# A two-layer decoder with a hand-ordered instruction list: filler matmuls in the last part of TensorE's list, and new orders for four engines

## The chip, the cores and the metric

The kernel runs on one core of a Trainium2 chip. A core has four engines that compute, each with its own instruction queue worked off strictly in order: TensorE (PE, matmuls and transposes; PEld is its weight load), VectorE (DVE), ScalarE (ACT) and GpSimd (POOL). SyncE (SP) issues the DMAs. They synchronise by semaphores alone. The metric is the device time of one execution in microseconds, lower is better.

## The reference

Input are 32 sequences of 128 rows with 256 channels, and a context of the same shape. Six sublayers follow each other, each as x = layernorm(x + f(x)):

```python
x = _layernorm(x + _L0_attn_ref(x, ...))        # 16 heads, window of 7 keys, extra weights per window place
x = _layernorm(x + _L0_xattn_ref(x, ctx, ...))  # one-head attention on the context
x = _layernorm(x + _L0_ffn_ref(x, ...))         # 8 experts, each takes its 16 best rows, attends among them
x = _layernorm(x + _L1_attn_ref(x, ...))        # one-head attention, scores times a decay mask
x = _layernorm(x + _L1_xattn_ref(x, ctx, ...))  # row of context chosen by argmax, then 16-head attention
x = _layernorm(x + _L1_ffn_ref(x, ...))         # 256 -> 1024 -> conv of 3 -> silu -> 256, rounded to 8 bits / 3 values
```

All sequences are independent of each other until the end.

## The kernel before

The sequences are worked in 16 groups (`NG`) of two (`GB`), so a group is 256 rows. Every sublayer is a set of stations named by a letter: S setup (once), Q queries, keys and values and A the rest of the windowed attention; B cross attention; X and Y the two halves of the experts; C the decayed attention; D the choice of context rows and E the attention on them, T its output projection and norm; F the first part of the feed-forward, H its gating, second projection and norm. A station exists on each engine as a Python generator: at each `yield` it has issued one step, a few instructions with their semaphore waits and signals.

The order in which an engine issues steps is written out by hand as a string of letters in `ORDER`, one letter for a step. `walk` goes through it: a letter issues the next step of that station for its current group, and when a group's steps are used up, the station turns to the next group. So several groups are in flight at once, and what stands behind a waiting step in an engine's string waits with it.

I name a step by its letter, its group and its work. For TensorE these are, in the last part of its string:

- D15.kv, D15.xT, D15.q, D15.sc, D15.hotT, D15.v: projections, transposes and scores of the choice of group 15, in PSUM bank_c.
- E15.sc0, sc1 (scores of the two sequences, line 868), negT (transpose of the row maxima, line 876), lg0 and lg1 (logits, lines 889 and 893), val0 and val1 (values, in line 904's loop), tu0 and tu1 (turned back, line 909). E15.sc0 waits for `d_v_out` at 16. In groups 14 and 15, lg1 waits for all four exponentials of lg0, val1 for those of lg1.
- T15.aT and T15.wc (lines 922 and 930): transposes and output projection; behind them the norm of T15: sums on VectorE (line 1027), squares on ScalarE (line 1535), scale on GpSimd (lines 1841 to 1847), normalisation on ScalarE (line 1542).
- F15.rows (line 936), xqT (line 955), p0 to p3 (line 966), and for the last group t0 to t3 (line 975): scale rows, transposes of the rounded rows, four projections that share bank_f, and four transposes of the gated result. VectorE reads a projection out (ev, line 1424), convolves it (line 1433), gates it (line 1443) and takes maxima (line 1463).
- H14.topT, H14.rows, H14.out (lines 990, 994 and 1012): maximum and scale of group 14's hidden values, then 16 matmuls. VectorE makes the four parts that they read, n0 to n3 (line 1502). For group 15 there are H15.rows and four steps o0 to o3 of four matmuls (line 1005).

TensorE's string ends as follows, W aside: T14.wc, E15.sc0, H13.out, E15.sc1, F14.rows, F14.xqT, F14.p0, F14.p1, E15.negT, E15.lg0, F14.p2, E15.lg1, F14.p3, E15.val0, E15.val1, E15.tu0, E15.tu1, T15.aT, T15.wc, H14.topT, H14.rows, F15.rows, F15.xqT, F15.p0 to p3, F15.t0, F15.t1, H14.out, F15.t2, F15.t3, H15.rows, H15.o0 to o3.

The helpers `mm` (line 503), `project_rows` (line 513 its bias matmul), `to_channels` (534) and `turn_blocks` (539) issue most matmuls. `take` waits until a bank has been read out.

Of the kernel before, what the change touches and what calls it, by code (L numbers as in the profile page):

```python
# [67 lines left out]

ORDER = {
    "PE": (  # L70
        "QQQASSASASBQSQBAQAASDABABSBBQBQXBXASAXQXAXABXBABYBYQBYYYQYBAYAXQCXCABXBXAXBAXBQYCYQCYYYBYCAYCAXBXQDAXDXD"
# [1915 lines left out]
```

## Time and profile before

| | us |
|---|---|
| three runs | 1006.9, 1003.46, 1008.17 |
| median | 1006.9 |
| the profiled execution | 1006.9 |
| its span, first to last instruction | 1005.1 |
| TensorE busy in the span | 915.2 (91%) |
| VectorE busy | 855.5 (85%) |
| ScalarE busy | 738.8 (74%) |
| GpSimd busy | 218.2 (22%) |
| TensorE's mean granted clock | 0.964 |

All times are microseconds. "Clock" is the clock that the chip granted to TensorE, as a share of 2.4 GHz; it knows two levels, 1.00 and 0.50, and a value between them is a mean over a stretch. Ends of matmuls are modelled, so a matmul is shown a little longer than it holds the queue; the distance from one start to the next is the better measure. In a timeline, square brackets give the idle time of the engine before a group, and what ended it.

### The profile page before, as it was taken

Reading aid. Unit: us, or ns where it says so; the run is one execution under the profiler, and the core shown is the slowest. Engines: PE = TensorE matmul, PEld = TensorE weight load, DVE = VectorE, ACT = ScalarE, POOL = GpSimd, SP = SyncE. Lnnn points to the kernel's source line nnn. Section 1 sums busy time; section 2 is a strip of 40 time slices with the busy share of each in tenths; the row PEclk is TensorE's granted clock in tenths of the full one; section 3 lists DMA queues with packets and bytes.
Section 4 is the critical chain, followed back from the end, with each engine's and each line's share of the span. In section 5 each row is a group of like instructions: output and inputs, shape, how many; then the busy total and the mean of one; then the engine's idle time right before and its main releaser. Section 6 shows DMA issues by size and latency. Waiting matters only on the chain.

```text
span 1005.1 us, 20332 instructions
## 1 busy us (share of the span) xinstructions
PE 915.2 (91%) x7396; PEld 674.3 (67%) x7396; DVE 855.5 (85%) x2217; ACT 738.8 (74%) x1852; POOL 218.2 (22%) x469
## 2 busy tenths in 40 slices
PE   6888999999999999999999999999999999998654
PEld 4566676767777676767677676767677777665432
DVE  5787676599999999998999999989999997867776
ACT  2276556778887869877777878687878889878563
POOL 2012121303222231403122230313122222111101
PEclk9889999999999999999999999999999999999775
DMA  9932202020112103020302112030302100000000
GB/s 276 374 88 73 84 22 74 5 91 1 61 56 64 52 12 105 24 93 1 115 1 63 54 32 84 11 105 4 113 1 74 33 22 2 23 11 12 11 1 22
DMA packets 36628, 59.06 MB, mean 59 GB/s; under 512 B 6656, under 2 KB 15872, under 8 KB 36016
## 3 DMA queue, kind: packets, MB, share of 16 engines
q1 hardware_dynamic: 36528, 57.76, 18.3%
q8 instruction: 59, 0.97, 0.4%
q14 instruction: 41, 0.34, 0.1%
HBM read 28.77 MB, written 4.19 MB: 33 GB/s over the span
## 4 chain that ended last, share of the span: by engine, by line
PE 62%; ACT 16%; DVE 14%; POOL 3%; issue 3%; SPq 1%; DMA 0%; POOLq 0%; DVEq 0%; ACTq 0%
PE bank_c L503 17%; PE bank_a L503 8%; PE banks_e L503 7%; PE bank_x L503 7%; PE bank_x L714 4%; PE bank_f L503 4%; DVE neg_top L1355 3%; ACT area_e L1759 3%; PE banks_e L893 3%; PE bank_a L609 3%; ACT squares_out L1535 2%; ACT x L1542 2%; DVE area_f L1433 2%; ACT area_bx L1523 2%; PE bank_c L534 2%
## 5 line engine op out<-in xcount | busy, mean ns | idle before, releaser
L1433 DVE SCALAR_TENSOR_TENSOR area_f<-area_f,w_convw 128x254 f32<-128x254 f32 x240 | 104.7, 478 | 6.2 <-ACT area_f L1806 4.4
L1523 ACT ACTIVATE area_bx<-bank_x 128x512 f32<-128x512 f32 (+1 forms) x140 | 68.2, 499 | 23.7 <-PE bank_x L714 7.4
L1355 DVE TENSOR_REDUCE neg_top<-banks_e 128x8 f32<-128x1024 f32 x64 | 76.2, 1219 | 8.4 <-PE banks_e L503 8.1
L1149 DVE TENSOR_TENSOR area_a<-area_a 128x512 f32<-128x512 f32 x112 | 73.2, 683 | 2.6 <-PE bank_a L609 1.5
L1204 DVE TENSOR_TENSOR area_a<-area_a 128x512 f32<-128x512 f32 x112 | 74.5, 683 | 1.0
L1806 ACT ACTIVATE area_f<-area_f,w_convb,w_convw 128x256 f32<-128x256 f32 x120 | 65.4, 596 | 10.9 <-DVE area_f L1424 10.6
L1759 ACT ACTIVATE area_e<-banks_e 128x512 f32<-128x512 f32 x120 | 64.2, 602 | 9.5 <-PE banks_e L893 9.2
L1208 DVE TENSOR_TENSOR area_a<-area_a 128x512 f32<-128x512 f32 x96 | 65.7, 684 | 0.4
L1523 ACT ACTIVATE area_a<-bank_a 128x512 f32<-128x512 f32 (+1 forms) x80 | 44.0, 550 | 20.3 <-PE bank_a L503 15.7
L1523 ACT ACTIVATE area_bx<-bank_c 128x512 f32<-128x512 f32 x64 | 34.4, 538 | 27.1 <-PE bank_c L503 19.5
L503 PE MATMUL bank_x<-area_bx 128*128 128x128 f32 (+1 forms) x240 | 48.5, 335 | 3.9 <-ACT area_bx L1523 3.7
L1855 POOL TENSOR_TENSOR area_bx<-area_bx,minus 128x2 f32<-128x2 f32 x16 | 13.1, 819 | 179.0 <-ACT area_bx L1548 179.0
L503 PE MATMUL bank_f<-area_f,w1q 128*128 128x256 f16 x256 | 41.7, 289 | 7.6 <-DVE area_f L1424 5.7
L714 PE MATMUL bank_x<-w_wqkv_e,area_bx 128*32 128x384 f32 x512 | 47.9, 492 | 0.0
L1424 DVE TENSOR_TENSOR area_f<-bank_f,area_f 128x512 f32<-128x512 f32 x64 | 43.8, 685 | 4.5 <-PE bank_f L503 4.3
L503 PEld LDWEIGHTS bank_x<-area_bx 128*128 128x128 f32 x240 | 38.8, 193 | 10.8 <-ACT area_bx L1523 6.3
L1443 DVE SCALAR_TENSOR_TENSOR area_f<-area_f 128x512 f32<-128x512 f32 x60 | 41.0, 684 | 3.4 <-ACT area_f L1811 3.2
L1811 ACT ACTIVATE area_f<-area_f 128x512 f32<-128x512 f32 x60 | 38.0, 634 | 7.9 <-DVE area_f L1433 7.4
L503 PEld LDWEIGHTS bank_f<-area_f,w1q 128*128 128x128 f16 x256 | 23.0, 102 | 27.7 <-issue 10.5
L1523 ACT ACTIVATE area_e<-banks_e 128x512 f32<-128x512 f32 (+1 forms) x60 | 32.1, 536 | 10.9 <-PE banks_e L534 6.6
L609 PE MATMUL bank_a<-area_a,w_headsum 128*32 128x256 f32 x448 | 34.3, 386 | 5.7 <-DVE area_a L1149 5.2
L503 PE MATMUL banks_e<-chosen_key,chosen_q 32*128 32x256 f32 x512 | 36.7, 400 | 3.0 <-DVE neg_top L1355 1.8
(403 smaller groups left out, 2641.3 us busy)
## 6 DMA issues: line engine op xcount, KB each, us to landing
area_a<-area_a SPq DMA_DIRECT2D x96, 224.0 KB
area_a<-in_xT SPq DMA_DIRECT2D x16, 256.0 KB, 2.8
area_bx<-in_ctxT SPq DMA_DIRECT2D x16, 256.0 KB, 2.9
x<-in_x SPq DMA_DIRECT2D x16, 256.0 KB, 3.5
area_d<-in_ctxT SPq DMA_DIRECT2D x16, 256.0 KB, 2.7
y<-x SPq DMA_DIRECT2D x16, 256.0 KB, 2.2
w_wqkv_e<-in_wqkv_e SPq DMA_DIRECT2D x1, 3072.0 KB, 11.7
area_f<-in_raw SPq DMA_DIRECT2D x2, 1024.0 KB, 13.2
```

Source lines behind the costliest of these rows:

```text
L503: last = pe.matmul(out_ap, l, r, start=i == 0 and not opened, stop=closes and i == len(pairs) - 1)
L609: last = pe.matmul(bank_a[32 * j:32 * j + 32, 0:T], w["headsum"][:, at:at + 32], product_of(wi)[:, c * T:(c + 1) * T], start=wi % 2 + c == ...
L714: last = pe.matmul(bank_x[ES * q:ES * (q + 1), 0:3 * HP], xgf[:, c, e, :], wq[:, c, e, :], start=c == 0, stop=c == DC - 1)
L1149: return dve.tensor_tensor(product_of(wi).rearrange("p (n t) -> p n t", t=P), qT0.rearrange("p c (b t) -> p (c b) t", t=P), kT0.rearrange( ...
L1204: made[wi] = own.mark(dve.tensor_tensor(v4, v4, bc(e4[:, :, wi, :], 3, DH), ALU.mult))
L1208: added = dve.tensor_tensor(vw[:, to, :], vw[:, to, :], vw[:, wi, :], ALU.add)
L1355: dve.tensor_reduce(top[:, b, r:r + 2, :, 0].rearrange("p r (par c) -> p r c par", c=DC), banks_e[:, r:r + 2, :].rearrange("p r (c par k) ...
L1424: dve.tensor_tensor(blocks(th_f[jj % 3], 2), blocks(bank_f[:, :], 2), bc(tscale_f, 1, 2), ALU.mult).then_inc(f_h, 1)
L1433: last = dve.scalar_tensor_tensor(c4[:, i, :, dst], h4[:, i, :, src], cwt3[:, 2 * jj + i, k:k + 1], c4[:, i, :, dst], ALU.mult, ALU.add)
L1523: return act.activation(dst, src, ACT.Copy)
L1759: act.activation(weights(g, b)[:, r * 4 * P:(r + 1) * 4 * P], bank_e[r][:, :], ACT.Exp, scale=float(DH) ** -0.5).then_inc(e_exp, 1)
L1806: last = act.activation(c4[:, i], h4[:, i], ACT.Identity, bias=w["convb"][:, j:j + 1], scale=cwt3[:, j, 1:2])
```

## The change

Two things change. No matmul, vector or scalar operation of the computation is added or removed.

First, TensorE gets a station W, once, of 101 steps. A step is one matmul of the constant ones with a bias tile, 128 x 512 in bf16, into bank_c. Nothing reads the result. The station's first step has two waits.

```diff
+WARM = 101
...
-    left = {name: iter(range(1 if name == "S" else NG)) for name in stations}
+    left = {name: iter(range(1 if name in "SW" else NG)) for name in stations}
...
+            def warm(_):
+                pe.wait_ge(d_v_out, NG)
+                pe.wait_ge(n_e.added, GB * (LATE + 1))
+                for i in range(WARM):
+                    pe.matmul(bank_c[:, :], ones_bf[:, :], bc(bias_parts[0][:, :], 1, GB), start=True, stop=True)
+                    yield
```

`LATE` is 13, so the second wait is for the sum of x and group 13's output of station T, on VectorE.

Second, the strings of TensorE, VectorE, ScalarE and GpSimd are new; SyncE's is as before. The end of TensorE's:

```diff
-        "CHECYTHDTDXHDCDFXFDFXDFCEXECFCXFECECYYEEDYEDYHDHYEYDYDEDHTECTCECDFCFEFECFCFEEDFDDEEEDHTDHTEHEFFFFEEFEFEE"
-        "EETTHHFFFFFFFFHFFHHHHH"
+        "CEHCTYHDTDXHDDFFDFXDFXCECXEFCCXFCECEYEDYEEDYHDYHEYDEYDDHTTECCEFCFFCFEECFCEFDEDDEEDEHDTHDTWEHWWEWFWWFWFW"
+        "WWWFWWEWWWWWEWWWWWFWWWWWWWEWWFWWEWWWWWWWWWEWEWWWWWWWWEWWWWHTWHTWWHWWWWWFWWFWWWFWWWWFFWWWWWWWFWWWWWWWWWWF"
+        "WWWWWFWFWFWHWWHHWHH"
```

Decoded, with the number of fillers in brackets: T14.wc [1] E15.sc0, H13.out [2] E15.sc1 [1] F14.rows [2] F14.xqT [1] F14.p0 [4] F14.p1 [2] E15.negT [5] E15.lg0 [5] F14.p2 [7] E15.lg1 [2] F14.p3 [2] E15.val0 [9] E15.val1 [1] E15.tu0 [8] E15.tu1 [4] H14.topT, T15.aT [1] H14.rows, T15.wc [2] H14.out [5] F15.rows [2] F15.xqT [3] F15.p0 [4] F15.p1, F15.p2 [7] F15.p3 [10] F15.t0 [5] F15.t1 [1] F15.t2 [1] F15.t3 [1] H15.rows [2] H15.o0, H15.o1 [1] H15.o2, H15.o3.

The real steps that stand elsewhere here: H14.topT, H14.rows and H14.out are ahead of F15.rows, where H14.out was between F15.t1 and F15.t2. VectorE's maxima and gating of H14 and its norm move with them, ahead of F15's first projection, and ScalarE's squares of H14 stand behind F15's second convolution start. Further up, D15.kv stands behind F13.p3 instead of ahead of F13.rows, and C14.xT nine places later. In the rest of the strings the same steps change places with near ones: 445 of TensorE's 958 real steps stand at another place, 0.7 places away on average and 12 at most; 1057 of VectorE's 1629 (1.6 and 19), 815 of ScalarE's 1190 (1.3 and 18), and 64 of GpSimd's 160 (0.5 and 4).

## Rows read from the trace of the kernel before

**Rows 1.** The page, part 1: busy us, share of the span, instructions.

```profile
PE 915.2 (91%) x7396; PEld 674.3 (67%) x7396; DVE 855.5 (85%) x2217; ACT 738.8 (74%) x1852; POOL 218.2 (22%) x469
```

**Rows 2.** Busy us and (x) instructions of each engine, granted clock, DMA, by stage.

```profile
200.00:900.00 700.00, 674.40 (x5758) 502.76 (x5747) 639.07 (x1667) 563.87 (x1434) 165.16 (x343) 1.00 0.15 47
900.00:937.00 37.00, 30.52 (x241) 22.42 (x241) 28.02 (x71) 28.59 (x68) 4.99 (x14) 0.91 0.03 8
937.00:1005.00 68.00, 37.51 (x251) 21.84 (x249) 49.02 (x114) 35.37 (x77) 7.31 (x22) 0.67 0.04 12
```

**Rows 3.** The same view, in stretches at which the granted clock changes.

```profile
915.40:918.80 3.40, 0.61 (x4) 0.31 (x4) 2.75 (x9) 3.26 (x10) 1.43 (x4) 0.99 0.00 0
...
929.10:932.30 3.20, 1.47 (x11) 1.01 (x12) 3.20 (x13) 1.83 (x4) 0.00 (x0) 1.00 0.00 0
...
942.70:946.10 3.40, 1.44 (x10) 0.73 (x10) 3.26 (x9) 2.66 (x8) 1.08 (x3) 0.99 0.00 0
946.10:959.70 13.60, 9.78 (x86) 5.16 (x90) 9.19 (x20) 9.39 (x19) 0.00 (x0) 0.50 0.06 20
959.80:970.20 10.40, 5.27 (x34) 2.96 (x26) 7.75 (x20) 6.45 (x14) 1.60 (x4) 0.99 0.00 1
970.30:990.50 20.20, 10.76 (x46) 6.41 (x47) 16.39 (x36) 9.82 (x18) 0.29 (x1) 0.50 0.01 1
...
994.00:1005.00 11.00, 3.98 (x18) 2.20 (x17) 3.79 (x9) 2.76 (x7) 1.47 (x5) 0.50 0.14 48
```

**Rows 4.** TensorE's instructions in order of time: start, us, line, output<-input, count.

```profile
901.50 1.89 PE L503 MATMUL bank_c<-w_wc1x,area_e 128*128 128x256 f32 x8
903.24 1.89 PE L503 MATMUL bank_a<-area_c,w_qk 128*128 128x256 f32 x8
...
906.13 0.39 PE L513 MATMUL bank_a<-bias_parts,ones_bf 128*128 128x512 bf16 x1
906.36 1.89 PE L503 MATMUL bank_a<-w_vp,area_c 128*128 128x256 f32 x8
...
911.95 0.40 PE L889 MATMUL banks_e<-area_e,w_quarters 32*128 32x128 bf16 x16
...
913.20 0.44 PE L539 MATMUL bank_a<-w_ident,area_c 128*128 128x128 f32 x2
...
928.01 1.06 PE L503 MATMUL banks_e<-area_bx,chosen_v 128*32 128x512 f32 x8
929.00 0.65 PE L539 MATMUL bank_x<-w_ident,area_e 128*128 128x128 f32 x4
```

**Rows 5.** The same view, the last 70 us.

```profile
939.01 1.92 PE L503 MATMUL bank_a<-w2q,area_f 128*128 128x256 f16 x16 [0.40 <-DVE area_f L1502]
...
947.60 0.64 PE L876 MATMUL banks_e<-w_ident,neg_top 128*128 128x128 f32 x2
...
965.27 1.99 PE L503 MATMUL banks_e<-w_wc1x,area_e 128*128 128x256 f32 x8 [0.69 <-ACT area_e L1523]
...
972.98 0.64 PE L936 MATMUL bank_f<-w_ident,area_f 128*128 128x128 f32 x2
```

**Rows 6.** The chain that ended last: start, us, engine and what.

```profile
973.19 0.44 PE bank_f L936 x2
...
977.21 1.04 PE bank_f L503 x4
...
987.83 3.07 PE bank_a L503 x16
990.92 0.90 DVE x L1027 x4
991.82 1.21 DVE area_a L1463 x2
```

**Rows 7.** VectorE's instructions in order of time.

```profile
978.28 0.69 DVE L1424 TENSOR_TENSOR area_f<-bank_f,area_f 128x512 f32<-128x512 f32 x1 [1.13 <-PE bank_f L503]
...
990.08 0.68 DVE L1443 SCALAR_TENSOR_TENSOR area_f<-area_f 128x512 f32<-128x512 f32 x1
```

More of the change, by code:

```diff
@@ new lines @@
+        "XDADXEBABYYEQBYCEBEQECYECEYCYECCAEYTDTDADXQDFAXDFDFABXEFBEXBFAXEBXEBFBYECQCEYCECQHYEYCEYHCYTDYTDXADHDADX"
+        "DFQEFBXFEXFBXBFEBEXFBACEBAYCAEYCQCEQYHEYCHYCEYDTYDTDHXADADXDFQEFBFEBAXBFXBXEFXBEBFAYCEYACQECYCEYQYHCECYD"
+        "EYDHTXDTDAHXADDQEFBFXEFBXBFXAEFBEFCXAACYEBBYECQCEYQYCHYEYECYTHDXTDHXDADADFDFQFXEBFEBXAFBEXBXFBAEBAYCEQCY"
+        "ECYECYHEDHEYCYCYTQTDAHXADXDQFDFDAEXBFEBXFBEXBXBFAEBYEFCEAYCQCYQCYECHYCYDYEXEDHATDTDHDAXDQFEFBFXEFBXBABXF"
+        "BEXEFABECYECAYCYQCYHEYQCYEHCEYTDXTADHDXDADDFEFBFXEBXFBQBXFAEBXFEBAECYACYECYECYQHECYHCEYDQTDYDTXDHDAXDABE"
@@ L81 @@
+        "FQFXEFBXBFEBXAFEBFXBAACECEYQCYECQYEYHCYEYTCTYDAXDHADXDHDQDAEFBFEXFBFXBABEXEFABBXCFEQEYCYECYCHYEYCEYTCYDX"
+        "HQDXTDHADADDFQXEFBFEFBXBABXBEFBEFCXEACAYECYECYYHDECYEHCYTBTYDHXDAXDFADFDFXFEXBEBXBXEBFBEYCCFEYECEYCYXYEY"
+        "CEHCTYHDTDXHDDFFDFXDFXCECXEFCCXFCECEYEDYEEYDYHDYHEYDEYDDHTTECCEFCFFCFEECFCEFDEDDEEDEHDTHDTWEHWWEWFWWFWFW"
+        "WWWFWWEWWWWWEWWWWWFWWWWWWWEWWFWWEWWWWWWWWWEWEWWWWWWWWEWWWWHTWHTWWHWWWWWFWWFWWWFWWWWFFWWWWWWWFWWWWWWWWWWF"
+        "WWWWWFWFWFWHWWHHWHH"
     ),
@@ L98 @@
-        "EEEFEFFFFFFFFFFFFFEEEEFFFFTFFHHFFHFHHHHFFFFFFFFFFFFFFFFFFHFFHHHHHHHHH"
+        "SSSQQQQSSASSSSSSAASSSSSSSAASSSSSASASASASAAAAAAAAAAASAAASSSSQSSSQSQQSSSSAASSSSSASASSSSSSSBBAASSSSASAAABAA"
+        "AAAAAAAAAAAAXXXSXSXXXXXAXQQQQXAAAYBBYYAAAAAABYYAAAAAAAAAAAAAAYAQQQQAXXXXXXXXXXAAXBBAAAAYYYABAAAAAYYAAAAC"
+        "CAAAAAAQQQQYCAAXXXXXXXXXXAADDDXYYYEEBBAAYYEEEEEEAAAAAAABAAAAAEEAAAAAACCCEQEYQQQTAAFFFDDDAAXXXXFXXXXXFXEE"
+        "FFEEEFEEEFFFBBFFYAYAYXBAAFFFFAFAEEFFFYAYFFCCAAHHAHAAAACEEAAAAAAYHHHHTQQQQHDDDFFFAXXAXXXXXXXEEFXEFEFFEEEE"
@@ new lines @@
+        "FFFFBBFFFFYYYAABFFFXFYYAAEFAAEFAACFFAACAAHHHAAAACEEAAAHHHHYATAQAHFFFDDDAQQQAXXXXXEEXXFXXEEXEEFEFFEBBFFFF"
+        "XYAAYYBFFFFAAYYFFFFAAAFFEEACACAFFAAAAAACAAAAEHHEHYAHHHQHAQTDDQQDHFAFXAXFXXXXXXXEEXEFEFEEFFEFEFFFBXBFFAAF"
+        "FYYYFFAAFAABFAYYFFEEFCCAFAAAAAAAAHAHAHEAAECAYHHHHATHQQFFQFDDDXXAQXXXXXXXAFEEFFFXEEEEEEFFFFBFBAAFFYFXYYBA"
+        "AFFFFFFYYEEAAAAAAFFCCAAHHHAAAAEAEAAACHHAHHAYTQQHQFAFQFADDXDXXXXXXXXAAEEFXEEEEEEFFFFBBFFFXYYYFFBFFAAFFFFY"
+        "YEEAAAAAFAFCCFFAAAACAAAAAHAYAHHAEEHHQQQHHTDDDQHAFXFFXXXXXXXXEEAFXEFFFEEFBEBEEFFFAAFFXFFYBYYFFFEEFAAYYFFA"
@@ new lines @@
+        "AAAFFCAHCAHHAAAAAAAAACEEAYAHHAHHTQQQQHDDDXFFFXXXXXXXAXEEXFEEEAFFFEFBBEEFFFFFAYAFFBYYFXFFFAAYEYFEFAAAAAFF"
+        "CCAAHAHHHHCAEHHAEAAAAYAAAAQTDDDQQXXQXXXHAFXXFXFXEEAXEFEEEFEEFFBBFXFFFFAAFFBFAAYYYAAFFFAAFAEEAAAYYFFCCFFA"
+        "AAEEAAAACAHHHAAYQTHHHHAAQQQDDDXXFXXXHFXXXAFXEEAEFXEEEFEEFFBBFFFFAAFBFFYYYFFFEEFFFFYYAAAAFXAFCCAAAEEAAAAC"
+        "HYHHAAAAAHHAHHXXQXTXXXHXXDDDFFFXAAQQQEEFEXEFFFFBBEEEEFFFXFBFFAAFFYYYFFFAAFFEEAYYFAFCCAHAAHHAAAEEHHCHHAAA"
+        "ATAAYAAAAHFFFDXDDXXXXXXAXXFXFEEFFXEEFEBEBEEFFYFYYBFFFFFEYEYFFFFFCCFFEEHHHCYHHHHTXXXXXHFFFDDDXXXXFXXFFFEF"
@@ new lines @@
+        "BCBYACYCXCXBAQDADXDXADDDXBYYBAYBQCYEEEEEBEQCBYCEEYEECCYEACTCDTDYATDQXYFFDXFDDDFAABFBFXBXEFFFBXEBEEEABEFC"
+        "FFQYCFBFCFEEYEECYEYCYCQYTDCDXYATDTHDFXDDDHFAFYBFQAXBFFBXEFFFBEEEXBECFFFBEAYCFFBAYCFQEEEEYCEYCYCYQDCTDYTD"
+        "TAHYXDXAFDDDFQFHBAFBBXFFXEBFXBFFEEEEYFCAEFFABCYFQFCBFYEEYECECEYCYDCQDYTDXTYATHDXDDDHAFFQFBAFBXFFXBFEFFEF"
+        "CEEEXABFFCABEYBFFYCFQBYCEEEYEYECYCTYDCXQDTHTDAYHXFDFADDDFQAFBBFXFFBXFEFBXAFBEEEEFFBECYFFAQCBYCFEEYEECYED"
+        "YCYCTQCYDATHTXDHXYFFDQDDDFABFABXBFEXFBFXFBFEEEEFAYECFFCABQYFFYCBFCYCEYECYEQECEDYDTXADTDTHXADDDFFHFYBAQFB"
@@ new lines @@
+        "BFXFFBXEFFBXFEEEEFFAECBYCFFYAFCYQBYCYEEEEYCECQTCYDDTXADTHXYDHDDDFFAFBFABBXFFQBXFFFEXBFEEEEAFFCEYBCAFFYFC"
+        "YEEEEYCCEQYCYDCQTDBYDXTDAXYDDDTHBAFFHFAQFBBXFEFBXFFFEBEEEXFACBAEFFFCYQBFCEEEYEFYCEYYCTYQCCDAXYDTDXATDQDD"
+        "DAHFFFBHFBYXBAFFEBXFEEBFFFEEXBCAFEFFBYFCEEFYCQYEEYCEYCYCDTCXDQYXDTATHDFDDDFAFHBAFYBQBFXFFBXEBFFEEEECFFXA"
+        "FEBCFFAYBFCYEEYECEYDECYCTYCBTDYXTDHXAFYFDFDDDFAAXBFFBXHFBEXBFFEECFBEECYEBFFYCEYEFFYEEXFYCECYTCDCYDTXTDYF"
+        "FFDFDDDXCFFHCXHFCFFCXCEFFFEEEEYCFFECDFYYDYEEEEYDEYDYDDDTYTCTCHFFFCHFECEFCFFEEECFFFCEFDFDEEFFEEFDEDTDDDTT"
@@ L113 @@
+        "FFFHFHEFFEEFEEFFFEEEFEFEFFEFTTTFFFFFHFFFFFFHHH"
     ),
     "POOL": (
-        "ABBABBYYABBYCCAYBBYCCTYABBYCCTHHYABBYHCCTAYHBBYCCYHTHABBYHCCTYHABBHYCCTYHABBYCCTHAYHBBYCCHTYHABBHYCCYTAH"
-        "BBYCCHTAHYBBYCCHTYHABBYCCHTHYABBYCCHYTHCCYYHHTCCHTHTHHHH"
+        "ABBABBYYABBYCCYABBYCCTAYBBYCHCTYHABBHYCCTYHABBYCCYTHHABBYCCHTYHABBYCCHYTHABBYCCHTHYABBCYHCYTHABYHCCBTYHA"
+        "BBYCCTHYAHBBYCCHTHAYBBYHCCTYHABBYCCYTHHCCHYYTHCCHTHTHHHH"
     ),
@@ L1015, in gate @@
                 yield
-            walk(ORDER["PE"], {"H": gate, "Y": combine, "T": connect, "S": setup, "Q": queries, "A": windowed, "B": cross, "X": experts, "C": decayed, "D": choose, "E": memory, "F": feed_forward})
+            def warm(_):
[4 more added lines that the diff above has]
+                    yield
+            walk(ORDER["PE"], {"W": warm, "H": gate, "Y": combine, "T": connect, "S": setup, "Q": queries, "A": windowed, "B": cross, "X": experts, "C": decayed, "D": choose, "E": memory, "F": feed_forward})
         @block.vector
```

39 lines of the change are left out of this document (4 added, 35 removed).

## The prediction

> **What bounds the kernel now.** I read the page first for the shares of busy time [rows 1], then the busy time and clock by stage [rows 2], then the last 90 us in the stretches at which TensorE's clock changes [rows 3], then TensorE's own instructions in order of time [rows 4, 5], and last the chain of waits and VectorE's instructions at the end [rows 6, 7].
>
> The body is bound by TensorE. From 200 to 900 us it is busy for 674.40 of 700 us at full clock, VectorE for 639.07 [rows 2], so all waits together come to 25.6 us there. The stretch from 900 to 937 holds 6.5 us of idle TensorE at clock 0.91, and the last 68 us hold 30.5 at a mean clock of 0.67 [rows 2]. That last part is where this change has most to win: no other groups are left to fill the queue, the chain goes in turn through VectorE, ScalarE and TensorE, and TensorE's share of it runs partly at half clock (1.2 GHz, the granted 0.50).
>
> What TensorE did before each fall stands in [rows 3]. Before the fall at 918.8 it was busy for 0.61 of 3.4 us, before that at 932.3 for 1.47 of 3.2, before that at 946.1 for 1.44 of 3.4. Over 959.8 to 970.2 it was busy for half the time and then fell too. Half clock holds from 946.1 to 959.7, from 970.3 to 990.5 and from 994.0 to the end.
>
> **The fillers' size.** The nearest row is the bias matmul, which has the same operands, shape and type: it starts at 906.13 and the next instruction at 906.36, so it holds the queue for 0.23 us at full clock, though shown as 0.39 because ends are modelled [rows 4]. 101 fillers are 23.2 us. They begin behind T14.wc, at about 937, and TensorE is idle for 30.5 us after that [rows 2], so on the whole they fit. At half clock one is at most 0.46 us. Their two waits add nothing: `d_v_out` at 16 is what E15.sc0, the next real step, waits for anyway, and the sum of group 13 was done long before. Nobody reads bank_c after it.
>
> The Trainium skill (TensorE: Matmul & The Clock Gate, Wait — 56ns, not 53.3ns?) gives 215.7 ns start to start for 512 columns at full clock; the row shows 0.23 us, near it. By the page's figure all 101 would be an estimated 21.8 us, 1.4 us less than by the row.
>
> **Step 1: 900 to 937 us.** D15.kv (eight matmuls; by the 1.74 us of eight with 256 columns [rows 4], some 1.0 us for its 144) moves from in front of F13.rows, where the queue is full, to behind F13.p3, so it comes near the hole at 915.4, where TensorE does 0.61 us in 3.4 [rows 3]. It can win its own 1.0 us. If it keeps the clock from falling at 918.8 or 932.3, it wins up to 1.7 more each time (half of 3.4 us). Lower bound: nothing, if ScalarE's copy of it then holds up the copies behind it (D15.xT, D15.q, the exponentials of E14). I take 1.5, with 0 to 3 kept.
>
> **Step 2: T14.wc to E15.negT, 13 fillers.** They are 3.0 us beside about 7 us of real work in the 12 us up to 947.6. The chain here is mostly VectorE's (factors of H13, norm of T14, the two maxima of E15), so they hide; a clock that does not fall at 946.1 saves a few tenths on F14.p1, and four fillers ahead of it give them back. I take 0.
>
> **Step 3: E15.negT to the end of T15.wc, 44 fillers.** This took from 947.60 to 967.26 (965.27 + 1.99) [rows 5]: 19.7 us. Real work at full clock, by start-to-start distances in [rows 4]: the two logit steps 1.25 each (911.95 to 913.20), the two value steps 0.99 each (928.01 to 929.00), a turn of four blocks 0.50 (0.65 less the 0.15 by which ends overrun: 901.50 + 1.89 against 903.24), three such (tu0, tu1, aT), three of two blocks 0.25 (negT, topT, H14.rows), two projections of F14 0.44 each (the sixteen matmuls at 939.01 hold 1.92 - 0.15 [rows 5], so 0.11 each), and wc 1.74. Sum 2.5 + 1.98 + 1.5 + 0.75 + 0.88 + 1.74 = 9.35. The 44 fillers add 10.1. So the queue itself cannot pass this stretch in less than 19.5 us, against 19.7: the clock saves several us on real matmuls, and the fillers spend them. T15.wc also waits for ScalarE, which must do two rounds of four exponentials between F14's steps, and for VectorE, which now finishes the maxima of F14 and starts H14 before T15's norm. I take 0. Bounds: 1.0 gained, if fillers go faster; 1.5 lost, if the nine ahead of E15.val1 (2.1 us) or the eight ahead of E15.tu1 (1.8 us) outlast the wait that they stand in.
>
> **Step 4: H14.out goes ahead of F15.** It now lies in the 5.7 us between T15.wc and F15.rows (967.26 to 972.98) [rows 5]: norm of T15, squares, scale, normalisation on three other engines. Two fillers, 1.77 of H14.out and five fillers are 3.4 us; VectorE must first make n2 and n3, some 1.3 us, and TensorE still ends before F15's scale is there. So the move costs nothing; with that cover gone it would cost 1.8. Before, it was on the chain: 3.07 us at half clock, with VectorE's four pieces of H14's norm, 0.90, behind it, and the last two maxima, to 993.03 (991.82 + 1.21) [rows 6]. VectorE had finished the last gate of F15 at 990.76 (990.08 + 0.68) [rows 7]. Now only the transposes of F15.t3 (1.1 at half clock) and one maximum (0.6) follow that gate: 992.5. Gain 0.5; 0.9 at full clock. Only ScalarE's squares of H14 are now in front of F15's first tanh, 1.1 us that its gate has slack for.
>
> **Step 5: the front of F15.** Four TensorE pieces of the chain between 973.19 and 977.21, 3.14 us at half clock, and H14.rows ahead of them [rows 6]: at full clock 1.7 to 1.9 less, minus 0.1 to 0.2 for the fillers that overrun (two, three and four of them in front of xqT, p0 and p1, in waits of about 0.5, 0.7 and 0.8). From F15.ev1 at 978.28 to 990.76 VectorE runs almost without a gap [rows 7], so this stretch only shifts. I take 1.7, bounds 1.0 and 1.9.
>
> **Step 6: the last matmuls.** After F15.t0 the fillers get thin: five, one, one, one and two, against gates that end some 3 us apart. The stretch then looks like 942.7 to 946.1, and I expect the clock to be at half again for H15: no gain. If it holds, H15.rows and the sixteen last matmuls (3.98 us busy from 994 on [rows 3]) save about 1.6, plus the 0.4 of step 4.
>
> The Trainium skill (TensorE: Matmul & The Clock Gate, Part 4: PE-mode transpose) says that transposes are not counted as a busy TensorE. The rows that bear on it are those before 932.3, 1.47 us of little but transposes, and they agree without proving it. By that rule F15.t0 to t3 would hold nothing up and H15 would lose the 2.0 us; without it step 6 might go either way.
>
> **Step 7: the order of all engines.** Of 958 real steps of TensorE 445 stand at another place in its queue, by 0.7 places on average; VectorE's 1057 of 1629, ScalarE's 815 of 1190. The work is the same. With 25.6 us of waits in 700 [rows 2], 15% of them either way is 4 us. No reason excludes a sign. At the start DMA and group 0's chain set the pace, and the swaps that I followed (Q1's last product ahead of A0's norm; A0's normalisation behind a setup copy) weigh 0.3 to 0.7 us against each other. I take 0, plus or minus 4.
>
> **Sum:** 1.5 + 0 + 0 + 0.5 + 1.7 + 0 + 0 = 3.7 us off the profiled execution's 1006.9 (span 1005.1 and 1.8 around it), which equals the median of the three runs: 1003.2.
>
> **Rivals.** (a) The clock holds to the end, and fillers run a little faster than the row: 3.7 + 2.0 + 1.0 = 6.7 us less, 1000.2. For it: fillers occupy most idle time until F15.t0. Against it: the thin end. (b) The new order takes waits out of the body: 15 to 20% of 25.6 us more, some 4.5, with the 3.7: about 998.7. Nothing in the trace excludes it. (c) Slower: one swap in the body is bad and repeats for each group. An engine's queue is strict, so a step placed in front of one whose input comes first costs a wait; ScalarE's mean instruction is 0.40 us (738.8 over 1852 [rows 1]). At sixteen groups and 0.6 us, a copy and a half, that is 9.6, less 3.7: 1012.8. It decides from 0.55 us per group on (8.7 us, which leaves 5 slower). TensorE at 96% has no slack to hide it; against it, VectorE's 91% and the short moves. (d) The fillers do not keep the clock up, or get in the way: steps 4 to 6 shrink to 0.5, and step 3 pays twice for fillers at half clock. All of its 44 at half clock would add 10, but so full a queue was followed by full clock at 959.8, so I price one such stretch of 3.4 us, 1.7, and 1.5 of misplaced fillers: with step 1, 1006.9 - 2.0 + 3.2 = 1008.1.
>
> **How the numbers follow.** About 0.5%, 5 us, is what a measurement of this kernel can tell from no change: its runs spread over 4.7. Forecast 0.38, own range 999.5 to 1006.5; (a) 0.25; (b) 0.11; (c) 0.13; (d) 0.13. Faster: 0.07 of the forecast's, 0.22 of (a) and 0.11 of (b), 0.40. Slower: (c) 0.13 and 0.03 of (d), 0.16. The rest, 0.44, is the same. The range 996 to 1009 leaves out most of (c) and the outer parts of (b).
>
> **What would show it.** Right: clock 1.00 from 937 to about 985; E15.negT to T15.wc still 19 to 20 us; H14.out behind T15.wc at full clock; VectorE without a wait from F15.ev1 on; half clock at H15; busy time of 200 to 900 us as before. Wrong: E15's stretch much shorter or longer than 19.7 (step 3), idle time in the body changed by over 4 us (step 7), full clock in the last 10 us (step 6).

## The result, and the profile after

The change makes the kernel slower: 1013.6 us (median of 5 runs, 1012.94 to 1014.0) against 1004.4 (5 runs beside it, 1003.46 to 1008.17), a ratio of 1.0081 with a 95% interval of 1.0058 to 1.0102 (it weighs all runs; the two medians alone would give 1.0092). The forecast was 1003.2, the range ended at 1009.

The profiled execution took 1010.35, span 1008.4: only 3.4 over the one of before, where the medians are 9.2 apart. Before's own profiled execution was a late one (2.5 over the median of the runs beside this one), that of after an early one (3.3 under). So a place in the trace is compared below by how much its distance to the trace of before changes, and the times between kernels are taken from the rounds.

The page, part 1, of the changed kernel [rows 1 are those of before]:

```profile
PE 924.4 (92%) x7497; PEld 674.0 (67%) x7497; DVE 856.6 (85%) x2217; ACT 735.8 (73%) x1852; POOL 215.5 (21%) x469
```

The 101 fillers are there (7497 instructions of TensorE against 7396), and the other engines have the same counts. The view by stage, as in [rows 2]:

```profile
200.00:900.00 700.00, 671.16 (x5689) 497.98 (x5689) 634.06 (x1647) 557.94 (x1421) 160.06 (x339) 1.00 0.15 46
900.00:937.00 37.00, 30.12 (x248) 21.51 (x247) 27.49 (x68) 29.50 (x72) 6.08 (x17) 0.95 0.05 16
937.00:1008.00 71.00, 53.90 (x382) 30.46 (x380) 53.27 (x127) 36.44 (x82) 7.41 (x23) 0.95 0.04 12
```

In the 700 us of the body TensorE gets through 69 instructions fewer than before (5689 against 5758) and is idle for 3.2 us more, 28.8 against 25.6, though the clock is 1.00 in both and there is no filler in it. In the last row the clock is 0.95, where it was 0.67. So the clock of the end went as forecast and the body did not. The granted clock in the last 71 us, with the stretches cut where it changes, as in [rows 3]:

```profile
937.00:994.20 57.20, 47.93 (x351) 26.93 (x349) 45.93 (x111) 33.24 (x75) 5.86 (x18) 1.00 0.02 5
994.20:997.70 3.50, 2.82 (x10) 1.77 (x10) 2.91 (x5) 1.51 (x3) 0.00 (x0) 0.52 0.22 75
997.70:1004.50 6.80, 3.15 (x21) 1.76 (x21) 4.02 (x12) 1.09 (x4) 0.90 (x4) 0.99 0.01 2
```

Full clock until 994.2, half for 3.5 us, full for 6.8; behind it no matmul is left. TensorE's instructions in order of time, as in [rows 5] (E15.negT, T15.wc, two fillers, H14.out, five fillers, F15.rows, and later F15.t2):

```profile
953.25 0.38 PE L878 MATMUL banks_e<-w_ident,neg_top 128*128 128x128 f32 x2
...
971.70 1.99 PE L505 MATMUL banks_e<-w_wc1x,area_e 128*128 128x256 f32 x8
973.52 0.59 PE L1023 MATMUL bank_c<-bias_parts,ones_bf 128*128 128x512 bf16 x2
975.75 1.92 PE L505 MATMUL bank_a<-w2q,area_f 128*128 128x256 f16 x16 [1.64 <-DVE area_f L1511]
977.51 1.24 PE L1023 MATMUL bank_c<-bias_parts,ones_bf 128*128 128x512 bf16 x5
979.17 0.43 PE L938 MATMUL bank_f<-w_ident,area_f 128*128 128x128 f32 x2 [0.42 <-DVE area_f L1423]
...
994.72 1.11 PE L977 MATMUL banks_e<-w_ident,area_f 128*128 128x128 f32 x4 [2.03 <-DVE area_f L1452]
```

From E15.negT to the end of T15.wc it is 953.25 to 973.69 (971.70 + 1.99), 20.4 us. H14.out lies behind T15.wc at full clock. The chain that ended last, as in [rows 6], with VectorE's part where [rows 7] had its gates:

```profile
983.38 0.69 DVE area_f L1433
...
994.06 0.61 DVE area_f L1452
994.72 1.11 PE banks_e L977 x4
...
996.26 0.87 PE banks_e L977 x4
997.15 0.70 DVE area_a L1472
```

The gate at 994.06 is the third of F15's four and releases F15.t2. The last one stands in VectorE's instructions in order of time (F15.ev1, the last gate, the last maximum):

```profile
983.38 0.69 DVE L1433 TENSOR_TENSOR area_f<-bank_f,area_f 128x512 f32<-128x512 f32 x1 [0.70 <-PE bank_f L505]
...
995.18 0.68 DVE L1452 SCALAR_TENSOR_TENSOR area_f<-area_f 128x512 f32<-128x512 f32 x1
...
997.15 0.69 DVE L1472 TENSOR_REDUCE area_a<-banks_e 128x2 f32<-128x512 f32 x1 [0.59 <-PE banks_e L977]
```

VectorE works without a wait from F15.ev1 (983.38, line 1433; line 1424 before) to the end of the last gate at 995.86: 12.5 us, as much as in [rows 7] (978.28 to 990.76). Behind the last gate the chain holds only F15.t3 and one maximum, 2.0 us until 997.84; before, with H14's norm between them, it was 2.3 us until 993.03.

Where the time was lost shows when the same step is looked up in both traces, each counted from its first instruction. After less before, in us: group 2's turned input of the experts (X2.xT, at 142) -1.9; A13.val (695) -0.8; X15.xT (844) +1.3; T12.wc (854) +3.6; C14.xT +10.7, its new place counted in; C15.xT (901.0 to 909.0) +8.0; E15.negT +5.6; F15.rows +6.2; H15.o3, the last product, +3.8. So 9.9 us are lost between X2.xT and C15.xT, 8.8 of them behind 695 us, and 4.2 are won back from there to the end. The loss is ahead of 909 us, where only the order was changed, which step 7 had put at 0. Of the 8.8 us 4.6 are shown as idle time of TensorE; the rest is shown as busy, with ten more instructions between the two places and with modelled ends, so a sum of waits doesn't account for all of it.

In 800 to 900 us TensorE was busy for 93.19 us before and for 90.43 after. Two places of that stretch, before, TensorE in order of time: first C14.vp, F12.p2, C14.sc; then T13.aT, E14.sc0, C15.xT, which T13.wc and C15.qk follow at 901.50 and 903.24 [rows 4]:

```profile
870.53 1.89 PE L503 MATMUL bank_a<-w_vp,area_c 128*128 128x256 f32 x8
872.25 0.60 PE L503 MATMUL bank_f<-area_f,w1q 128*128 128x256 f16 x4
873.10 1.16 PE L503 MATMUL bank_a<-area_c 128*128 128x128 f32 x8 [0.25 <-ACT v_c L1523]
...
899.41 0.60 PE L534 MATMUL bank_c<-w_ident,area_e 128*128 128x128 f32 x4
899.94 1.15 PE L503 MATMUL banks_e<-chosen_key,chosen_q 32*128 32x256 f32 x16
901.01 0.66 PE L534 MATMUL bank_a<-w_ident,x 128*128 128x128 f32 x4
```

And the same steps after, C14.vp and C14.sc, then T13.aT, T13.wc, E14.sc0, C15.xT, C15.qk:

```profile
874.78 1.89 PE L505 MATMUL bank_a<-w_vp,area_c 128*128 128x256 f32 x8
877.35 1.16 PE L505 MATMUL bank_a<-area_c 128*128 128x128 f32 x8 [0.69 <-ACT v_c L1532]
...
904.66 0.60 PE L536 MATMUL bank_c<-w_ident,area_e 128*128 128x128 f32 x4
906.04 1.97 PE L505 MATMUL bank_c<-w_wc1x,area_e 128*128 128x256 f32 x8 [0.78 <-ACT area_e L1532]
907.94 1.15 PE L505 MATMUL banks_e<-chosen_key,chosen_q 32*128 32x256 f32 x16
909.01 0.66 PE L536 MATMUL bank_a<-w_ident,x 128*128 128x128 f32 x4
910.36 1.99 PE L505 MATMUL bank_a<-area_c,w_qk 128*128 128x256 f32 x8 [0.69 <-ACT area_c L1532]
```

C14.sc needs what ScalarE reads out of C14.vp's bank. Before, F12.p2 stood between them and the wait was 0.25; after, F12.p2 is ahead of both and the wait 0.69. T13.wc needs ScalarE's copy of T13.aT, and C15.qk that of C15.xT; before, E14.sc0 and C15.xT stood behind T13.aT and T13.wc behind C15.xT, and none waited. After, the pairs stand side by side and TensorE waits 0.78 and 0.69. I call such a step in between a cover.

### The profile page after: what moved, and what is told of

The parts are those of the page before. It is cut to its first block, busy times and chain, and to the rows that moved or that the text cites. A ratio compares the mean times of both kernels' runs of the same rounds, so it can differ in the third digit from the quotient of the medians.

```text
span 1008.4 us, 20535 instructions
## 1 busy us (share of the span) xinstructions
PE 924.4 (92%) x7497; PEld 674.0 (67%) x7497; DVE 856.6 (85%) x2217; ACT 735.8 (73%) x1852; POOL 215.5 (21%) x469
## 4 chain that ended last, share of the span: by engine, by line
PE 60%; ACT 17%; DVE 14%; issue 3%; POOL 3%; SPq 2%; DMA 1%; DVEq 0%; POOLq 0%; ACTq 0%
PE bank_c L505 16%; PE banks_e L505 8%; PE bank_a L505 8%; PE bank_x L505 6%; PE bank_f L505 3%; PE bank_x L716 3%; ACT area_e L1768 2%; PE banks_e L895 2%; ACT area_bx L1532 2%; ACT squares_out L1544 2%; PE bank_a L611 2%; ACT x L1551 2%; DVE area_f L1442 2%; DVE neg_top L1364 2%; PE bank_c L536 2%
## 5 line engine op out<-in xcount | busy, mean ns | idle before, releaser
L505 PE MATMUL bank_f<-area_f,w1q 128*128 128x256 f16 x256 | 39.1, 276 | 3.1 <-DVE area_f L1433 1.9
L505 PE MATMUL bank_a<-area_a,w_wq 128*128 128x256 f32 x128 | 34.0, 413 | 5.8 <-DMA w_wq<-in_wq 4.1
L505 PE MATMUL bank_c<-area_bx 128*128 128x128 f32 (+1 forms) x192 | 36.2, 324 | 3.2 <-ACT area_bx L1532 2.9
```

Of the source, the lines that this page charges most:

```text
L505: last = pe.matmul(out_ap, l, r, start=i == 0 and not opened, stop=closes and i == len(pairs) - 1)
```

## The experiments

Each was timed in rounds with the kernel before on the same chip; all ratios are to that. "Old" and "new" are the orders of before and after. Where the expectations number the theories, P3 is the one far move of C14.xT as the cause, and P4 the covers that the new order takes away from between a step and the one that needs its read-out.

**Order or fillers, and which part of the order.** Four kernels. First the new order without the 101 fillers (`WARM = 0`, every W out of the string):

> The new orders of all four engines, without the 101 fillers and their two waits. Theory P (the loss comes from the new order ahead of 935 us, and the tail, fillers included, wins some 2 us): 1.011 to 1.016 of the kernel before, so 1015 to 1020 us, a little slower than the changed kernel's 1013.6, with the clock at half for some 30 us after 935. Rival Q (the fillers cost the time, the order is harmless): 1004 to 1006 us. Rival R (both are harmless, and the clock's phase at the start makes the difference): within 0.3% of the kernel before.

Measured: 1016.9, 1.0116 (1.0090 to 1.0141). The fillers are not the loss; they give back about a third of one that is larger, 11.7 us.

The old order with the fillers, ahead of the same steps (here the front of F15 and the steps of H14 stay where they were):

```diff
-"...EHTECTCECDFCFEFECFCFEEDFDDEEEDHTDHTEHEFFFFEEFEFEE"
-"EETTHHFFFFFFFFHFFHHHHH"
+"...EHTECTCECDFCFEFECFCFEEDFDDEEEDHTDHTWEHWWEWFWWFWFW"
+"WWWFWWEWWWWWEWWWWWFWWWWWWWEWWFWWEWWWWWWWWWEWEWWWWWWWWETTWWWWHWHWWWWWFWWFWWWFWWWWFFWWWWWWWFWWWWWWWWWWFWWW"
+"WWFWWHWFWFWHWWHHWHH"
```

> The orders of before on all engines, with the 101 fillers in front of the same real steps as in the changed kernel (H14.out stays between F15.t1 and F15.t2). Theory P: full clock after 937 us until about F15.t1, E15.negT to T15.wc still 19 to 20 us, the front of F15 1.7 us shorter: 1001 to 1004 us, 0 to 0.3% faster than before. Rival Q: 1010 to 1014 us, slower by most of the 9 us.

Measured: 1006.0, 1.0002 (0.9989 to 1.0015). Full clock for most of 937 to 975 us and no gain, where theory P expected up to 0.3%: from the start of T15.wc to F15.rows it is 9.5 us (967.06 to 976.59) where [rows 5] have 7.7, since the five fillers ahead of F15.rows begin only behind H14.rows, which waits until 974.28. A filler behind a late step is itself late.

New order until 745 us, old behind it, no fillers; and old until 935 us, new behind it, with fillers (the cut is where the strings of all engines have done the same steps):

> On each engine the changed kernel's order up to what it had begun by 745 us, the rest in the order of before, no fillers. By the two traces the new order is level with the old one at 745 us when the start is counted (-1.1) and has lost 1.5 to 2 us since 60 us. If the loss sits mostly between 745 and 912 us (theory P1): 1004 to 1007 us. If it is spread over the whole body or sits before 745 (P2): 1009 to 1012 us.

> On each engine the order of before up to what it had begun by 935 us, then the changed kernel's order with its 101 fillers and H14.out ahead of F15. Theory P: the tail alone is the part of the change that wins: 1001 to 1003 us, 0.1 to 0.4% faster than before. Rival Q: 1008 to 1014 us.

Measured: 1007.1, 1.0015 (1.0000 to 1.0030), and 1004.8, 0.9998 (0.9983 to 1.0014). The start costs 0.15%, with an interval that touches 0, and the end with its fillers is level, not 0.1 to 0.4% faster as theory P had it. So most of the loss should lie from 745 to 935.

**Inside 745 to 935.** The new order in one stretch alone, 745 to 850 or 850 to 935, the rest old, no fillers:

> Order of before, except for what the engines begin between 745 and about 850 us, which goes by the changed kernel's order; no fillers. In the changed kernel's trace this stretch loses 4.4 us (T12.wc from -0.9 at 745 us to +3.6). If the loss is made there and carried to the end (theory P1a): 1008 to 1010 us, 0.3 to 0.5% slower. If the groups that come after make up for it (P1b): within 1.5 us of the kernel before.

> Order of before, except for what the engines begin between 850 us and the step T14.wc, which goes by the changed kernel's order; no fillers. Here C14.xT stands nine places later and D15.kv twelve. By the traces T14.wc stands 1.9 us later against T12.wc than before, C15.xT 4.4 later. P1a: 1007 to 1009 us. If the moved C14.xT is the seat of the loss (theory P3): 1010 us or more, since the last groups' chain starts there.

Measured: 1009.3, 1.0041 (1.0024 to 1.0058), and 1009.3, 1.0041 (1.0027 to 1.0055). The loss is in both, so it is not one place. TensorE in the first of them, around 790 and 845 us (C12.vp's bias, Y13.av; Y14.pickT, E12.val1, Y14.up):

```profile
786.07 0.39 PE L514 MATMUL bank_c<-bias_parts,ones_bf 128*128 128x512 bf16 x1 [0.67 <-ACT area_c L1714]
...
791.85 0.71 PE L504 MATMUL bank_x<-area_bx 128*128 128x128 f32 x4 [0.58 <-ACT area_bx L1531]
```

```profile
843.62 0.66 PE L750 MATMUL bank_a<-w_ident,picked 128*128 128x128 f32 x4 [0.60 <-ACT area_bx L1531]
844.60 1.07 PE L504 MATMUL banks_e<-area_e,chosen_v 128*32 128x512 f32 x8 [0.32 <-ACT area_e L1767]
846.09 1.07 PE L504 MATMUL bank_a<-w_wo_e,area_bx 128*32 128x256 f32 x16 [0.43 <-ACT area_bx L1531]
```

Five waits, 2.6 us together, all for what ScalarE reads out of a step close ahead (before Y13.av its turned input is the neighbour in front); in the trace of before none of the five steps waits. They are picked out: the trace of before has waits in this stretch that this one lacks (0.86 at 832.52, 0.57 at 837.52), and this one has others. Over the same steps, from the last keys' product (`w_wk`) to T12.wc, TensorE takes 106.4 us where it took 103.1, and is idle for 6.1 where it was for 3.4. This is where the groups run out: in the trace of before the last product of the windowed attention starts at 811.96. That fewer chains are then left to put between two steps of one is my reading and was not tested.

**C14.xT.** It and D15.kv are the two steps between 745 and 935 us that the new order moves far. The old order with it moved to its new place, and the changed kernel with it moved back:

```diff
-"CHECYTHDTDXHDCDFXFDFXDFCEXECFCX..."
+"CHECYTHDTDXHDDFXFDFXDFCCEXECFCX..."
...
-"FCFHDFDDDXHCFFFX..."
+"FFHDFDDDXCHCFFFX..."
```

> Order of before with one step moved: C14.xT behind F12.p1 on TensorE (from behind D13.q), and its copy behind X15.xg on ScalarE. Nothing else changes. P3 (the chain C14, Y15, C15, D15, E15 sets the end, and its start was put off by 10.8 us): 1007 to 1010 us. If the step has slack there (P1a, the loss is spread over many small waits): 1005 to 1006.5 us, the same as before.

> The changed kernel, fillers and all, with C14.xT and its copy put back where the kernel before has them (behind D13.q, and behind F12's first copy on ScalarE). P3: 1007 to 1010 us, against the changed kernel's 1013.6. If the loss is spread: 1012 to 1014.5 us.

Measured: 1007.8, 1.0023 (1.0011 to 1.0034), and 1014.7, 1.0102 (1.0081 to 1.0124). The first is inside what P3 expected, and its trace shows why it costs: C14.qk now stands right behind C14.xT and waits 1.2, and D13.sc, which C14.xT had stood in front of, waits 0.7 instead of 0.25. The second is no gain at all. So the late start of C14 is not the cause in the changed kernel; there E13.sc0 stands between C14.xT and C14.qk, which doesn't wait, and only D13.sc's 0.7 is left. In the old order the move costs; that it does so by these two waits is read from the trace.

**The covers alone.** The old order of every engine, with three moves in TensorE's string: F12.p2 ahead of C14.vp, E13.tu1 and T13.wc to their new places.

```diff
-"CHECYTHDTDXHDCDFXFDFXDFCEXECFCXFECECYYEEDYEDYHDHYEYDYDEDHTECTCECDF..."
+"CHECYTHDTDXHDCDFXFDFXDFCEXEFCCXFECECYYEEDYEDYHDHYEYEDYDDHTTECCECDF..."
```

> Order of before on all engines, no fillers, with three moves in TensorE's string alone: T13.wc directly behind T13.aT, F12.p2 ahead of C14.vp, E13.tu1 ahead of D14.sc, so that T13.wc, C15.qk, C14.sc and D14.v each follow the step whose read-out they need, with nothing between. Theory P4 (the loss is a sum of TensorE waits of one read-out, 0.5 to 0.8 us, at steps that lost what stood between them and what they need, and TensorE has no slack until about 915 us): four waits, 2.7 us, so 1007 to 1008 us, 0.2 to 0.3% slower. If waits are absorbed further on (rival): 1004 to 1005.5 us.

Measured: 1009.5, 1.0036 (1.0016 to 1.0055), as much as the whole new order of 850 to 935. TensorE in order of time, C14.vp and C14.sc, then T13.aT, T13.wc, E14.sc0, C15.xT, C15.qk:

```profile
869.52 1.89 PE L504 MATMUL bank_a<-w_vp,area_c 128*128 128x256 f32 x8
872.10 1.16 PE L504 MATMUL bank_a<-area_c 128*128 128x128 f32 x8 [0.69 <-ACT v_c L1531]
...
898.79 0.60 PE L535 MATMUL bank_c<-w_ident,area_e 128*128 128x128 f32 x4
900.30 1.97 PE L504 MATMUL bank_c<-w_wc1x,area_e 128*128 128x256 f32 x8 [0.91 <-ACT area_e L1531]
...
904.62 1.99 PE L504 MATMUL bank_a<-area_c,w_qk 128*128 128x256 f32 x8 [0.69 <-ACT area_c L1531]
```

(E14.sc0 and C15.xT are the lines left out ahead of the last.) The waits stand at the same three places as in the changed kernel, 0.69, 0.91 and 0.69; with 0.47 ahead of D14.v and 0.45 ahead of C15.vp's bias they are 3.2 us, of which before had 0.25. Against before this trace moves from -1.4 (ahead of C14.vp) to +2.0 (C15.vp, 908.37 against 906.36 in [rows 4]), 3.4 us; the timed loss is 3.6. No other engine's order was touched. This is what P4 said in kind; it had priced four waits at 2.7 us, 1007 to 1008.

**The covers given back.** The kernel above with the new order from 850 to 935 alone, with two moves in TensorE's string, F12.p2 back behind C14.vp and T13.wc back behind C15.xT; in the second kernel ScalarE's copy of C15.xT also goes ahead of T13's squares:

```diff
-"...FXCECXEFCCXFCECEYEDYEEYDYHDYHEYDEYDDHTTECCEFC..."
+"...FXCECXECFCXFCECEYEDYEEYDYHDYHEYDEYDDHTECTCEFC..."
```

```diff
-"...DYDDDTYTCTCHFFFC..."
+"...DYDDDTYCTTCHFFFC..."
```

> The kernel with the changed order between 850 us and T14.wc only (1009.3 us, 4.1 over before, in its own job), with two moves in TensorE's string alone that put cover back: T13.wc behind C15.xT and F12.p2 behind C14.vp. P4: three waits of 0.7 to 0.8 us go, 1.5 to 2.2 us of 4.1: 1006.5 to 1008 us. Rival (what counts is the place of the last group's steps on VectorE and ScalarE): no change, 1009 us.

> As new_850_covers_back (T13.wc behind C15.xT, F12.p2 behind C14.vp on TensorE), and on ScalarE the copy C15.xT ahead of T13's squares. If cover works only where all strings agree (P4 as it now stands): the wait of 2.2 us at C15.qk goes to nothing and those of 0.7 at T13.wc and C14.sc stay away, so 1.5 to 2.2 us less than the 4.1 of new_850_to_935 and some 4 less than new_850_covers_back: 1007 to 1008.5 us. If not: 1009 us or more.

Measured: 1012.0, 1.0070 (1.0049 to 1.0092), and 1012.8, 1.0081 (1.0062 to 1.0099): both above the 1.0041 that they were to mend, the second clear of its interval. I had expected 1.5 to 2.2 us less. The wait at C14.sc is gone (0.25 again), and T13.wc starts without one. But in the first, TensorE (T13.wc, C15.qk) and ScalarE (the norm of x ahead of C15.xT, the squares of T13, the copy of C15.xT):

```profile
904.44 1.89 PE L504 MATMUL bank_c<-w_wc1x,area_e 128*128 128x256 f32 x8
908.53 1.99 PE L504 MATMUL bank_a<-area_c,w_qk 128*128 128x256 f32 x8 [2.19 <-ACT area_c L1531]
```

```profile
902.82 1.08 ACT L1550 ACTIVATE x<-x,bn_scale_x 128x256 f32<-128x256 f32 x2
906.90 0.51 ACT L1543 ACTIVATE squares_out<-x,bn_sums_e 128x256 bf16<-128x256 f32 x1 [3.00 <-DVE x L1035]
...
907.90 0.57 ACT L1531 ACTIVATE area_c<-bank_a 128x512 f32<-128x512 f32 x1
```

ScalarE's string has the squares of T13 ahead of C15.xT's copy, and they need T13.wc by way of VectorE. With T13.wc later, ScalarE waits 3.00 for them, and TensorE 2.19 for the copy behind them. In the second this wait is gone, and another of the same size stands one step on. TensorE (C15.qk, E14.sc1), and VectorE (the first of two pieces of T13's norm, which H12's norm follows, then the maxima of E14):

```profile
906.10 1.89 PE L504 MATMUL bank_a<-area_c,w_qk 128*128 128x256 f32 x8
910.21 1.90 PE L504 MATMUL banks_e<-chosen_key,chosen_q 32*128 32x256 f32 x16 [2.22 <-DVE neg_top L1363]
```

```profile
906.30 0.42 DVE L1035 SCALAR_TENSOR_TENSOR x<-bank_c,x 128x256 f32<-128x256 f32 x1 [6.31 <-PE bank_c L504]
...
907.80 2.35 DVE L1363 TENSOR_REDUCE neg_top<-banks_e 128x8 f32<-128x1024 f32 x2
```

VectorE's string has T13's norm ahead of E14's maxima; the maxima had their input for some 4 us. Putting a step back on TensorE was not free here: the other engines' strings had to agree with it. I didn't find a mended new order.

**The fillers.** The changed kernel without the 44 fillers of E15's stretch; the kernel with old order to 935 us with its fillers out; and the changed kernel once more, beside it:

> The changed kernel without the 44 fillers between E15.negT and T15.wc; the other 57 stay. Step 3 of the prediction said that this stretch is held by the queue, fillers included. If so and the clock holds by the real work and the fillers around: 1 to 2 us faster than the changed kernel, 1011.5 to 1012.6. If the clock falls in the stretch as before (13.6 us at half): 1014 to 1016 us.

> Order of before until 935 us, then the changed kernel's order with H14.out ahead of F15, without fillers. Fillers are worth 3.3 us in the new order by two jobs (1016.9 without, 1013.6 with). If they are worth as much here: 1007 to 1009 us, against 1004.8 with them. If the fillers bring nothing and the moved H14.out neither: 1004 to 1006 us.

> The changed kernel itself, on the chip of this job. 1012.5 to 1014.5 us, 0.7 to 1.0% over the kernel before.

Measured: 1015.0, 1.0097 (1.0077 to 1.0118); 1008.1, 1.0030 (1.0019 to 1.0042); 1012.4, 1.0074 (1.0055 to 1.0093). Without the 44 the clock falls at 962 us for 3.4 us and at 973 for 6.8, and nothing is won. With the old body, the new end is 0.30% slower without fillers and 0.02% faster with them. The last 68 us of those two kernels, without and with:

```profile
937.00:1005.00 68.00, 36.50 (x216) 20.59 (x216) 45.68 (x106) 33.75 (x73) 6.18 (x20) 0.64 0.04 12
```

```profile
937.00:1005.00 68.00, 47.58 (x319) 24.71 (x316) 45.74 (x106) 33.41 (x73) 6.54 (x20) 0.91 0.04 13
```

The clock is 0.64 and 0.91. So the fillers are worth 3.2 us there (1.0030 less 0.9998) and 3.5 to 4.2 in the changed kernel (1.0116 less 1.0081 or 1.0074). The intervals of the first pair don't overlap, those of the second just do.

**The best of both.** Old order until 935, the new end with 91 fillers, and D15.kv in the hole behind C15.pv, its copy behind the second convolution of F13:

```diff
-"...TECTCECDFCFEFECFCFEEDFDD..."
+"...TECTCECFCFEFECFCDFEEDFDD..."
...
-"...CTHCFFFDECFCEEEFCFEFCFFFDEE..."
+"...CTHCFFFECFCEEEFCFDEFCFFFDEE..."
```

> Order of before until 935 us, then the changed kernel's order with 91 fillers (five instead of nine ahead of E15.val1, four instead of eight ahead of E15.tu1, two instead of four ahead of H14.topT), and D15.kv with its copy moved from ahead of F13.rows to the hole behind C15.pv. P4: 1.0 us from D15.kv, up to 0.8 us from the fillers, on top of a tail that stood level with before within 0.15%: 1002 to 1004 us. If the copy of D15.kv holds up the exponentials of E14: 1004 to 1006 us.

Measured: 1004.1, 0.9986 (0.9972 to 1.0000). TensorE: C15.pv, D15.kv, F13.p2:

```profile
911.66 1.13 PE L505 MATMUL bank_a<-v_c,area_c 128*128 128x256 f32 x4
912.63 1.14 PE L505 MATMUL bank_c<-w_wkv1x,area_d 128*128 128x144 f32 x8
914.63 0.61 PE L505 MATMUL bank_f<-area_f,w1q 128*128 128x256 f16 x4 [0.86 <-DVE area_f L1433]
```

D15.kv fills the hole, 2.0 us between C15.pv and F13.p2 (912.63 to 914.63), all but 0.86. But F13.rows, which it had stood in front of, now waits 0.71 for VectorE and starts no earlier (906.45, against 906.35 in the kernel with old order to 935), and the two traces stay level to the end: E15.negT at 944.80 and 944.73, spans of 1001.1 and 1000.9. So neither the move nor the ten fillers less shows as a gain there. It has the lowest ratio of the study and beats the changed kernel by 0.9%; its interval and that of old to 935 overlap, and whether it beats the kernel before is not settled.

## Why the prediction was wrong

**Step 7 failed**: "I take 0, plus or minus 4". Timed stretch by stretch, the new order without fillers costs 1.5 us until 745, 4.1 from 745 to 850, 4.1 from 850 to 935 and 3.0 behind it, 12.7 together where all of it at once measured 11.7; each of the four has 1.2 to 1.7 either way, and the interval of the first touches 0. So the body, until 935, costs 9.7 where the step allowed 4. The step argued that the work is the same and that 15% of the waits either way is all that short moves can do. But the average of the waits does not bound what new waits add. Where a cover was taken from between a matmul and the one that needs its read-out, the trace shows a wait of 0.45 to 1.2 us, one ScalarE copy (0.5 to 0.6) and its hand-over, and from 868 to 908 us these went into the time in full: the same 313 matmuls from the scores ahead of C14.vp to C15.vp take 40.6 us instead of 37.1, 2.9 of the 3.5 more as idle TensorE. Averages such as "0.7 places away" can't see that; the string can, if one lists every step whose input comes from the step just ahead of it. The covers' share is shown for 850 to 935, where three moves alone cost 3.6. For 745 to 850 it is read from the trace and not undone, and how much each wait weighs stays open. So does the start until 745.

**Rival (c)** had the side, the price (0.6 us, "a step placed in front of one whose input comes first costs a wait") and almost the time, 1012.8. That its 9.6 us are close to the 9.7 is luck: it had one swap repeated over sixteen groups, where there are several different ones between 745 and 935 us. With 0.13 it had too little: what spoke against it, VectorE's 91% and the short moves, is no protection.

**Step 1** (gain 1.5): from C15.xT to E15.negT the distance to before shrinks by 2.4, with the clock at 0.95 instead of 0.91. Whether D15.kv's move brought it is not shown; tried in the old order, it only moved the wait to F13.rows.

**Steps 2 to 6** are best seen together, in three traces that have the new end with all fillers. The place less that of before, in us:

| place (before) | changed kernel | changed kernel, second trace | old to 935, new end |
|---|---|---|---|
| T14.wc (935.53) | +5.5 | +8.1 | -3.3 |
| T15.wc (965.27) | +6.4 | +9.0 | -2.1 |
| F15.rows (972.98) | +6.2 | +8.7 | -2.3 |
| F15.ev1 (978.28) | +5.1 | +7.6 | -3.4 |
| end of the last gate (990.76) | +5.1 | +7.6 | -3.4 |
| end of the last maximum (993.03) | +4.8 | +7.3 | -3.8 |
| H15.o3 (997.79) | +3.8 | +7.3 | -3.8 |

Steps 2 and 3 (0 each) were in their bounds, but lost 0.9 to 1.2 us. E15's stretch is 20.4 us, where it was 19.7 and the forecast said 19 to 20. The reason given, a queue full of fillers, is not what holds it: with ten fillers fewer it is 20.4 us too (944.80 to 965.23 in the last kernel above), 17.9 of it busy, and H14.topT, which the new order has ahead of T15.wc, waits 1.09 for VectorE. The 44 fillers hold the clock for what comes behind.

Step 5 (1.7, bounds 1.0 and 1.9) gained 1.1 in all three. Step 4 (0.5) gained 0.3 to 0.4: H14.out took its 1.92 at full clock and hid, though it waited 1.64 for VectorE's parts and with its five fillers ended only 0.42 ahead of F15.rows.

Step 6 (no gain) gained 1.0 in the profiled execution and nothing in the other two. In the first the clock fell at 994.2, behind 3.5 us in which TensorE was busy for 0.9, so that F15.t2 took 1.11 instead of 0.66, and it was full again for H15, from 997.7; in the other two it fell some 1.3 us later in the work, between F15.t2 and t3, and H15.o0 and o1 ran at half. The prediction named full clock in the last 10 us as a sign against this step. By the Trainium skill (TensorE: Matmul & The Clock Gate, Part 4: PE-mode transpose) transposes don't count as a busy TensorE. The fall doesn't need this rule, and the rise at 997.7 came after F15.t2, t3 and two fillers, eight transposes of ten matmuls; no run decides it.

So of the 2.2 us of steps 4 and 5 some 1.4 came, and steps 2 and 3 took most of that back. Timed with the old body, new end and fillers together give 0.2 us (1.4 worse to 1.7 better), and without fillers the new end costs 3.0, which no step had priced. So of the gap between forecast and result 9.7 us are step 7's and some 2 us the other steps'.

**Rival (d)** did not come in the changed kernel as priced, but did in the old order with fillers, where they stood in the way for 1.8 us.

## What to carry to other kernels

In a kernel with fixed strings, ask of every new neighbour pair on the engine that is the bound: does the second need what another engine reads out of the first? Each such pair costs one read-out and hand-over, here 0.45 to 1.2 us, in full where the bound has no slack. Look first at the last groups, where few other chains are left to stand in between. Fillers that hold TensorE's clock brought some 3 us here, ahead of steps that wait anyway, and nothing where five of them stood behind a step that was itself late; a move that looks free on one engine has to be followed through the strings of the others.

## What was not expected of the chip

Executions of one kernel differ by an offset that is there by 142 us and is then kept. The changed kernel was traced twice: X2.xT comes at 140.48 and at 143.26, and the product of a station T near 690 us at 689.81 and 692.49, in executions of 1010.35 and 1013.76 us. The granted clock fell at 18 and 59 us in both, but for 7.6 us in all in the first and 14.5 in the second; in the trace of before it fell at 18, 41, 59 and 89 us. In the eleven traces whose strings are those of before until 745 us, X2.xT lies between 139.51 and 143.92, and the runs of the kernel before spread from 1002.6 to 1008.5 in one batch. So a pair of profiled executions can hide more than half of a change of this size: here they are 3.4 us apart, and the medians 9.2.
